# A Mamba block with a mixture of experts on one core: all eight PSUM banks in one pool, and new places for the side steps

## What is computed

```python
xz = x @ in_proj_w.T;  x_ssm, z = split(xz)
x_conv = silu(causal_conv4(x_ssm, conv_w) + conv_b)
B, C, delta = split(x_conv @ x_proj_w.T);  delta = softplus(delta)      # 16, 16, 1 columns
for t:                                                                   # per feature d, state n
    h = exp(delta * A) * h + delta * B * x_conv
    y = sum_n h * C
y = (y + D_param * x_conv) * silu(z);  return y @ out_proj_w.T

probs = softmax(tokens @ router_w.T + router_b);  two best experts of 8, weights normalised
out = sum over the two: weight * (token @ expert_weights[e])
```

## Time and profile before

| | us |
|---|---|
| median of the runs | 2801.45 (2800.16 to 2802.34, 3 runs) |
| the profiled execution | 2800.39 |
| its span, first to last instruction | 2798.2 |
| mean granted clock of PE | 0.915 of full speed |

### The profile page before, as it was taken

One profiled execution on the slowest core, in us unless ns is written; L12 is line 12 of the kernel. 1 busy time (PEld: TensorE's weight loads), 2 busy tenths in 40 slices (PEclk: granted clock), 3 DMA queues, 4 the chain that ended last, 5 costly groups with the idle time before them and its releaser, 6 DMA issues.

```text
span 2798.2 us, 34482 instructions
## 1 busy us (share of the span) xinstructions
PE 2333.2 (83%) x9510; PEld 1349.9 (48%) x9510; DVE 2258.4 (81%) x3144; ACT 1487.9 (53%) x2417; POOL 1808.3 (65%) x1418
## 2 busy tenths in 40 slices
PE   5668677698989989798988889798988989798886
PEld 2335344455545455454545455454545555454442
DVE  3789988989898989898888989888888989767300
ACT  3554555466564656466564656566474656434221
POOL 2556766657575867768676767768685767748542
PEclk8778877899999999899999999899998999899998
DMA  3772421223233443435443443435353443346866
GB/s 121 252 270 85 143 82 39 99 72 127 87 115 107 132 134 112 143 98 151 117 136 103 131 136 110 146 99 144 113 149 100 126 142 104 119 121 181 223 209 154
DMA packets 192569, 366.27 MB, mean 131 GB/s; under 512 B 22912, under 2 KB 22912, under 8 KB 192384
## 3 DMA queue, kind: packets, MB, share of 16 engines
q1 hardware_dynamic: 144272, 263.26, 28.8%
q0 software_dynamic: 28672, 67.13, 11.2%
q10 hardware_dynamic: 19440, 33.69, 3.3%
HBM read 212.73 MB, written 151.26 MB: 130 GB/s over the span
## 4 chain that ended last, share of the span: by engine, by line
PE 34%; DVE 20%; issue 18%; ACT 12%; POOL 12%; DMA 3%; SPq 0%; DVEq 0%; POOLq 0%; ACTq 0%
PE work L1191 11%; PE work L1195 10%; DVE h L1020 9%; DVE acc L1028 7%; PE hT L1206 6%; POOL u L735 5%; DVE xc L1051 3%; ACT decay L881 3%; PE work L1206 3%; PE work L1186 2%; POOL x_out L835 2%; POOL row_scratch L820 1%; POOL row_scratch L822 1%; ACT L881 1%; ACT xc L933 1%
## 5 line engine op out<-in xcount | busy, mean ns | idle before, releaser
L735 POOL TENSOR_TENSOR u<-xc,b_ring 128x1024 f32<-128x1024 f32 x512 | 1221.0, 2404 | 758.0 <-DVE h L1020 554.0
L881 ACT ACTIVATE decay<-dt,neg_a 128x512 f32<-128x512 f32 x1024 | 699.1, 689 | 603.2 <-DVE h L1020 581.3
L1206 PE MATMUL hT<-ident,h 128*128 128x128 f32 x4096 | 681.6, 298 | 349.2 <-DVE acc L1028 252.4
L1206 PEld LDWEIGHTS hT<-ident,h 128*128 128x128 f32 x4096 | 513.1, 152 | 683.2 <-DVE acc L1028 311.7
L1020 DVE TENSOR_TENSOR_SCAN h<-decay,h_last,u 128x512 f32<-128x512 f32 x512 | 651.6, 1274 | 131.8 <-ACT decay L881 85.5
L1020 DVE TENSOR_TENSOR_SCAN h<-decay,u 128x512 f32<-128x512 f32 x512 | 620.5, 1214 | 137.5 <-ACT decay L881 92.2
L1028 DVE SCALAR_TENSOR_TENSOR acc<-hT,ct,acc 128x512 f32<-128x512 f32 x960 | 697.1, 726 | 20.6 <-PE hT L1206 19.2
L1191 PE MATMUL work<-w_exp,xeT 128*128 x764 | 385.2, 628 | 34.0 <-issue 20.8
L1195 PE MATMUL work<-w_exp,xeT 128*128 x764 | 360.5, 594 | 0.0
L1191 PE MATMUL work<-xnT,w_in 128*128 128x512 f32 x512 | 261.9, 637 | 0.7 <-issue 0.7
L1195 PE MATMUL work<-xnT,w_in 128*128 128x512 f32 x512 | 241.9, 595 | 0.0
(11 more groups left out here) (149 smaller groups left out, 2193.6 us busy)
## 6 DMA issues: line engine op xcount, KB each, us to landing
b_ring<-b_scratch SPq DMA_DIRECT2D x256, 256.0 KB
xe<-row_scratch SPq DMA_DIRECT2D x165, 256.0 KB
result_scratch<-ye SPq DMA_DIRECT2D x165, 256.0 KB
row_scratch<-x_out ACTq DMA_DIRECT2D x32, 1024.0 KB, 4.7
x<-in_x SPq DMA_DIRECT2D x66, 256.0 KB, 5.1
x_scratch<-x SPq DMA_DIRECT2D x64, 256.0 KB, 2.1
xn<-in_x SPq DMA_DIRECT2D x62, 256.0 KB, 3.9
x_out<-x_scratch SPq DMA_DIRECT2D x44, 256.0 KB, 3.3
```

The lines of the kernel that those rows point to most:

```text
L735: nc.gpsimd.tensor_tensor(out=u[:, at:at + 2, :], in0=xc[:, half, 2 * k:2 * k + 2, :], in1=b_ring[:, n % ROWS:n % ROWS + 1, :].to_broadcas ...
L881: nc.scalar.activation(decay_bank[g % 2][:], dt[:, half, :], ACT.Exp, scale=neg_a[:, c, n:n + 1]).then_inc(decay_ready, 1)
L1206: last = nc.tensor.transpose(ps[:, k * P:(k + 1) * P], tile(k), ident[:])
```

## The change

One pool of eight banks takes the place of the three sets. `OWNERS` says which use a bank last had: two decay, two transposes, four products at the start. `choose` picks a bank among the idle ones. A decay or a transposed state takes one of its own, or one of the products' as long as it owns fewer than three (`RINGS` gives the least and the most). A product takes one of the products', else an idle one of a use that owns more than two, else any idle one. The first of the idle list is the one that has been free longest. What a bank's next user waits for is that bank's own last use (`wait_bank`): a scan, a sum, or a product's release. The order of `decay`, `scan`, `h_sum` and `h_T` in the list stays. The numbers of all eight tables are new; a few are shown.

```diff
@@ -52,129 +52,131 @@
     PLACES = N * C + 3
-    WORK = 4
+    BANKS = 8
+    OWNERS = ["decay"] * 2 + ["h_T"] * 2 + ["work"] * 4
+    RINGS = {"decay": (2, 3), "h_T": (2, 3)}
     HT = 2
...
-        "gather": [8.51, 14.25, 31.61, 33.76, 45.59, 48.95, 54.3, 62.45],
+        "gather": [8.8, 12.29, 29.08, 31.46, 41.89, 47.71, 54.7, 60.67],
-        "y_T": [3.7, 4.51, 4.55, 4.82],
+        "y_T": [4.43, 4.52, 4.87, 4.87],
-        "y_skip": [5.86, 5.98, 7.73, 9.62],
+        "y_skip": [5.75, 5.85, 7.57, 7.79],
-        "y_gate": [9.95, 10.13, 10.35, 10.44],
+        "y_gate": [6.67, 6.71, 10.4, 10.55],
-        "out_project": [10.17, 11.89, 14.71, 15.84],
+        "out_project": [10.75, 11.89, 14.71, 15.84],
-        "norm_stat": [4.74, 5.93, 12.25, 15.81],
+        "norm_stat": [5.92, 7.34, 15.35, 15.62],
-        "norm_rstd": [9.64, 19.17],
+        "norm_rstd": [10.21, 19.08],
-        "norm_apply": [7.43, 12.34, 18.05, 18.16],
+        "norm_apply": [10.01, 10.14, 18.01, 18.99],
-        "conv": [24.42, 25.32, 26.7, 27.51, 28.22, 29.02, 29.17, 31.14, 33.61, 34.98, 35.28, 35.75],
+        "conv": [25.96, 26.63, 26.77, 29.89, 30.06, 30.69, 33.81, 34.1, 35.13, 35.88, 36.01, 36.4],
-        "z_evict": [47.03, 49.21, 59.5, 61.93],
+        "z_evict": [48.82, 49.67, 57.75, 60.86],
-        "silu_x": [37.83],
+        "silu_x": [38.14],
-        "dt_exp": [42.94],
+        "dt_exp": [43.99],
-        "dt_plus": [42.67],
+        "dt_plus": [43.66],
-        "b_scale": [44.08],
+        "b_scale": [43.97],
-        "row_of": [40.91],
+        "row_of": [38.98],
-        "expert": [12.67, 15.33, 18.98, 27.8, 33.16, 35.02, 40.91, 47.06, 52.1, 58.89, 61.63, 65.09],
+        "expert": [13.29, 15.09, 20.77, 27.8, 32.16, 35.02, 40.91, 47.18, 52.65, 58.89, 62.04, 66.25],
-        "expert_end": [13.41, 15.35, 19, 28.22, 33.16, 35.04, 40.93, 47.08, 54.79, 58.91, 62.38, 66.67],
+        "expert_end": [14.16, 16.45, 20.89, 28.62, 33.06, 35.44, 42.33, 49.08, 56.19, 60.91, 62.38, 68.25],
-        "expert_evict": [15.73, 17.5, 23.7, 31.49, 37.48, 39, 47.74, 55.35, 58.65, 63.34, 66.63, 68.35],
+        "expert_evict": [17.5, 19.88, 25.42, 34.04, 37.55, 39.98, 51.57, 57.23, 60.02, 64.58, 67.09, 71.31],
...
@@ -294,33 +296,65 @@
 
     TAKES = {"norm_T": "norm_evict", "project": "project_out", "z_project": "z_evict", "dt_project": "dt_plus", "xp_project": "b_scale",
              "c_T": "c_evict", "y_T": "y_skip", "out_project": "residual", "norm2_T": "norm2_evict",
-             "router": "gate_logits", "rank": "row_of", "rows_T": "rows_evict", "expert": "expert_evict"}
-
-    def frees(s):
+             "router": "gate_logits", "rank": "row_of", "rows_T": "rows_evict", "expert": "expert_evict",
+             "decay": "scan", "h_T": "h_sum"}
+
+    def held(j, s):
+        if s[0] == "h_T":
+            return ("h_sum", ((j + s[3]) * N + s[1]) * Q + s[2])
+        if s[0] == "decay":
+            return ("scan",) + s[1:]
+        return TAKES[s[0]], s[1]
+
+    def frees(j, s):
+        if s[0] == "h_sum":
+            return ("h_sum", ((j + s[3]) * N + s[1]) * Q + s[2])
+        if s[0] == "scan":
+            return s
         if s[0] == "conv" and s[2] == EDGE - 1:
             return ("project_out", s[1])
         return s[:2]
 
-    def work_banks():
-        uses, idle, count, holder = {}, list(range(WORK)), [0] * WORK, {}
+    def choose(idle, owner, s):
+        of = s[0] if s[0] in RINGS else "work"
+        if of == "work":
+            long = [r for r, (least, _) in RINGS.items() if owner.count(r) > least]
+            some = [i for i in idle if owner[i] == "work"] or [i for i in idle if owner[i] in long]
+        else:
+            may_grow = owner.count(of) < RINGS[of][1]
+            some = [i for i in idle if owner[i] == of or may_grow and owner[i] == "work"]
+        i = (some or idle)[0]
+        owner[i] = of
+        return i
+
+    def bank_uses():
+        uses, idle, holder = {}, list(range(BANKS)), {}
+        count, last, owner = [0] * BANKS, [None] * BANKS, list(OWNERS)
         for j in ITERATIONS:
             for s in iteration(j):
                 if s[0] in TAKES:
                     assert idle, (j, s)
-                    bank_no = idle.pop(0)
-                    uses[j, s] = bank_no, count[bank_no]
-                    count[bank_no] += 1
-                    holder[TAKES[s[0]], s[1]] = bank_no
-                elif frees(s) in holder:
-                    idle.append(holder.pop(frees(s)))
+                    i, key = choose(idle, owner, s), held(j, s)
+                    idle.remove(i)
+                    uses[j, s] = i, count[i], last[i]
+                    if s[0] == "h_T":
+                        uses[key], last[i] = i, ("summed", key[1])
+                    elif s[0] == "decay":
+                        last[i] = "scanned", (j * N + s[1]) * C + s[2] + 1
+                    else:
+                        count[i] += 1
+                        last[i] = "free", count[i]
+                    holder[key] = i
+                elif frees(j, s) in holder:
+                    idle.append(holder.pop(frees(j, s)))
         return uses
 
-    USES = work_banks()
+    USES = bank_uses()
     STEP_IN = {(s[0], s[1]): j for j in ITERATIONS for s in iteration(j) if s[0] in EXPERTS}
 
     def use_of(j, key):
         j = STEP_IN.get(key, j)
-        return USES[j, key]
+        return USES[j, key][:2]
 
     ctx = ExitStack()
     with ctx:
@@ -429,17 +463,15 @@
         def bank(name):
             return ctx.enter_context(nc.psum_tensor(name, [P, 512], fp32))
 
-        decay_bank = [bank(f"decay{i}") for i in range(2)]
-        hT_bank = [bank(f"hT{i}") for i in range(HT)]
-        work_bank = [bank(f"work{i}") for i in range(WORK)]
+        work_bank = [bank(f"bank{i}") for i in range(BANKS)]
 
         b_dram = nc.dram_tensor("b_scratch", [2, N, T], fp32, kind="Internal").ap()
         x1_dram = nc.dram_tensor("x1_scratch", [TOKENS, D], fp32, kind="Internal").ap()
         row_dram = nc.dram_tensor("row_scratch", [2 * REGION, D], fp32, kind="Internal").ap()
         res_dram = [nc.dram_tensor(f"result_scratch{i}", [RESULTS, D], fp32, kind="Internal").ap() for i in range(3)]
 
-        work_full = [sem(f"work_full{i}") for i in range(WORK)]
-        work_free = [sem(f"work_free{i}") for i in range(WORK)]
+        work_full = [sem(f"work_full{i}") for i in range(BANKS)]
+        work_free = [sem(f"work_free{i}") for i in range(BANKS)]
         first_loaded = [sem(f"first_loaded{i}") for i in range(Q)]
         project_loaded = sem("project_loaded")
         scan_loaded = sem("scan_loaded")
@@ -561,6 +593,24 @@
             else:
                 wait(eng, summed, (block * (N - 1) + m - 1) * Q + q + 1)
 
+        def decay_bank(j, n, c):
+            return work_bank[USES[j, ("decay", n, c)][0]]
+
+        def hT_bank(k):
+            return work_bank[USES["h_sum", k]]
+
+        def wait_bank(eng, j, key):
+            i, _, last = USES[j, key]
+            if last is None:
+                return
+            kind, n = last
+            if kind == "scanned":
+                eng.wait_ge(scanned, n)
+            elif kind == "summed":
+                wait_summed(eng, n // (N * Q), n // Q % N, n % Q)
+            else:
+                eng.wait_ge(work_free[i], n)
+
         def wait_full(eng, j, key):
             bank_no, before = use_of(j, key)
             eng.wait_ge(work_full[bank_no], before + 1)
@@ -876,9 +926,8 @@
                             wait_used(act, j - 1, ("dt_project", 0))
                         if j == 0 and n == 0 and c == 0:
                             act.wait_ge(a_ready, 2)
-                        g = n * C + c
-                        wait(act, scanned, j * N * C + g - 1)
-                        nc.scalar.activation(decay_bank[g % 2][:], dt[:, half, :], ACT.Exp, scale=neg_a[:, c, n:n + 1]).then_inc(decay_ready, 1)
+                        wait_bank(act, j, s)
+                        nc.scalar.activation(decay_bank(j, n, c)[:], dt[:, half, :], ACT.Exp, scale=neg_a[:, c, n:n + 1]).then_inc(decay_ready, 1)
                     elif s[0] == "h_sum" and s[1] == 0:
                         q, i = s[2], j + s[3]
                         k = i * N * Q + q
@@ -887,7 +936,7 @@
                             wait_used(act, i - 1, ("c_T", 0))
                             if j > 0:
                                 wait_product(act, j, ("y_T", C - 1))
-                        nc.scalar.activation(acc[:, q, :], hT_bank[k % HT][:], ACT.Copy, scale=ct[:, i % 2, q, 0:1]).then_inc(first_summed, 1)
+                        nc.scalar.activation(acc[:, q, :], hT_bank(k)[:], ACT.Copy, scale=ct[:, i % 2, q, 0:1]).then_inc(first_summed, 1)
                     elif s[0] == "keep_h":
                         n = s[1]
                         act.wait_ge(scanned, (j * N + n + 1) * C)
@@ -1017,7 +1066,7 @@
                             elif half == 1:
```

(13 more changed lines are left out.)

## The result

The changed kernel takes **2771.8 us** (median; 2768.6 to 2774.1) against 2800.8 for the kernel before in the same session: ratio 0.9891, 95% interval [0.9879, 0.9904]. It is faster by 1.1%. The prediction said 2815, slower; its range of 2760 to 2845 holds the time. All medians here are over fast runs; one slow run of e5, of 7314.73 us, is left out.

The account below looks back on a forecast made before the run. PE bounds an iteration from the gates to place 28, DVE with its stalls the rest. Iterations 3 to 14 +26, 0 to 2 -5, 15 and the end -6: total +15 on 2800.4 gives 2815 us, range 2760 to 2845.

Parts of the forecast that it names:

- rival A: Places 8 to 28: late ACT evictions, not PE, set the pace, so half the stalls return; 2760 us, chance 0.25.
- Iterations 0 to 2: Early iterations: a real third decay bank returns a third of 14 us of decay stalls; -5 us, bounds -14 to 0.
- Iteration 15 and the end: Last iteration and after: a quarter of ACT's 23.9 us wait for expert products returns; -6 us, bounds -24 to +13.
- Iterations 3 to 14: Twelve steady iterations: the part-by-part terms sum to +2.2 us each, +26 us in all.
- One-bank decays: Eight bare places outside the PE stretch pay 0.25 us each; +2.0 us an iteration, bounds 0 to 6.8.
- SiLU of x: Behind decay 38 instead of before it, one more place covers ACT's block; -1.5 us an iteration, bounds -2.3 to 0.
- Softplus: After decay 43: DVE stalls 1.3 us at dt_plus and 0.7 more at decay 44; +1.5 us an iteration, bounds 0 to 3.
- PE stretch: Places 12 to 28: PE is the bound with the same matmuls and keeps what stalls give back; 0 us.
- Gates: POOL's reordered queue around place 8 ends earlier or later by at most one gate, 1.25 us; 0 us.
- Third bank for transposed states: 23 of 64 transposed states get it, against DVE's 1.2 us wait; -0.5 us an iteration, bounds -1.2 to 0.
- B: Places 8 to 12: more PE work in places 4 to 7 keeps the clock high; 32 us less, 2783, chance 0.10.
- C: One-bank decays put ACT and DVE in lockstep, every eviction wait reaching DVE; 58 us more, 2873, chance 0.12.

Follow-up runs that it names:

- e5: Changed kernel with decays held to at most two banks, transposed states still up to three; 2766.7 us, ratio 0.9867 to the kernel before.
- e14: Changed kernel's pool with all old places, decays held at two banks, transposes two to three; 2777.0 us, ratio 0.9908 to the kernel before.
- e15: Changed kernel's pool with all old places and no ring allowed to grow beyond two banks; 2801.3 us, ratio 1.0000 to the kernel before.
- e1: Changed kernel with every table of places as before, so only the pool of eight banks is new; 2773.6 us, ratio 0.9895.
- e4: Changed kernel with the four steady tables (post, prep, experts, combine) as before, new late tables kept; 2774.6 us, ratio 0.9903.
- e7: Kernel before, with eight decays in each of iterations 3 to 14 made to wait for the scan just before; 2814.8 us, ratio 1.0063.
- e12: Changed kernel with old places in iterations 3 to 13, new ones in 0 to 2, 14 and 15; 2762.3 us, ratio 0.9853 to the kernel before.
- e8: Kernel before, with 27 decays in each of iterations 3 to 14 made to wait for the scan just before; 2869.2 us, ratio 1.0244.
- e16: As e12, with y_T, y_skip and y_gate at the changed kernel's places in iterations 3 to 13 too; 2763.0 us, ratio 0.9841.
- e6: Changed kernel with transposed states held to at most two banks, decays still up to three; 2898.3 us, ratio 1.0338 to the kernel before.
- e18: As e6, with the second load of expert rows at place 8.09 instead of 7.2; 2859.3 us, ratio 1.0200 to the kernel before.
- e3: Changed kernel with new steady tables and the late tables of before; no time, since its engines wait for each other in a circle.
- e13: As e12, with decays held at two banks and transposes allowed two to four; 2779.0 us, ratio 0.9908 to the kernel before.

## Why the prediction was right and wrong

It said 2815, slower, and the kernel got faster: the profiled span fell by 31.7 us where +15 was forecast. That the time lies within its range is owed to rival A's bound, not to the forecast.

**Iterations 0 to 2: the step that failed most.** It said -5 and the trace says -23. It credited only the third bank of the decays, with a third of their stalls, and put the third bank of the transposes at nothing here. By e14 and e15 14 of the 23 us come from that bank (434.6 against 448.8), by e1, e4 and the changed kernel 4 to 7 from the new places; for the decays' bank e5 and e14 leave 2.0 and 1.3, less than equal lists differ by. The step on the transposes' bank read DVE's wait for transposed states in iteration 8, 1.2 us, counted it for iterations 3 to 14 alone, and closed with "PE gains slack that nothing waits for". But in iterations 0 to 2 of the kernel before DVE waits 11.7 us for PE's transposes (6.1 for its sums, 5.6 for its scans), and 4.9 for the out projection, which is queued among them. These are the waits that e14 takes away. The stalls for decays, on which the prediction built, stay (28.9 us in e15, 27.6 in e14).

**Iteration 15 and the end: mis-sized.** -6 forecast, -18.4 measured (-18.2 and -0.2), within the bound of -24. The term was a quarter of ACT's wait for expert products, 23.9 us; that wait fell by 15.4, to 8.5, and 17.3 of the 18.2 us came between places 12 and 28. The pool gives up to 6.4 of it (e1, though e7 shows 3.9 with nothing changed there), the rest needs the new places there; new late tables alone don't bring it (e4, 180.2), all tables of iterations 14 and 15 do (e12, 168.5). The last run of expert tiles, which PE fills, did stay as it was: the gain lies before it.

**Iterations 3 to 14: the sign right, the size under half.** +26 forecast, +10.3 measured.

- *One-bank decays.* The mechanism was right and its price at a place nearly: 2.04 us from scan to scan (1558.21 to 1560.25 to 1562.29), 0.20 more, 0.25 forecast. That PE's stretch covers them is shown by e8 (1.0 us for 12 to 28). The term, +24, was too large: eight places at 0.20 are 19, and e7 measures 14.3 in the kernel before. A decay just ahead of an absence of ACT can cost far more, 4.0 us an iteration for places 36 to 40 of e8; with the SiLU in its new place the changed kernel doesn't pay that.
- *SiLU of x.* -1.5 an iteration forecast, and right: DVE's waits for decays in places 36 to 40 fell by 20.5 us, 1.7 an iteration. These places nevertheless grew by 20.5 us in all, since two taps and `row_of` came to stand there (29.4 us more busy time of DVE) and scans 38 now wait 8.7 us for POOL's `u`, which no term had. Waits for `u` fell by 10.2 in places 50 to 64.
- *Softplus.* Right: a stall of 1.26 us before `dt_plus` (1.3 forecast; the view names no one for it, and the logarithm ends 0.10 us before the step) and 0.48 before scan 44 (0.7). Places 42 to 44 grew by 21.8 us in the twelve iterations, 4.8 of it two one-bank decays; 17.0 are left, 18 were forecast. The drain that the Trainium skill counts with a table load (ScalarE: Activation LUTs, What ACT_TABLE_LOAD costs) is not in this trace either: the load ends at 1555.53 and the logarithm begins at 1555.54. Places 40 to 50 grew by only 9.7, though this term and seven one-bank decays were to bring 39: places 40 and 49 got shorter by 6.2 and 12.3 us (place 49 from 2.63 to 1.84 us in odd iterations and from 3.04 to 1.78 in even ones), which no term had.
- *PE stretch.* PE is the bound between places 12 and 28, as said (busy 27.07 of 27.07 and 20.09 of 20.09 us). But "the same matmuls" was counted by list places, not by time: more of them now run before scan 12, and the stretch lost 25.4 us in the sum. From scan 0 to scan 28 it is 5.7, near the 0 forecast. The sign that was to prove the prediction wrong, under 45 us, came in iterations 9, 11 and 13 (43.77 in iteration 9).
- *Gates.* 0 forecast, with "earlier or later by at most one gate", 1.25 us. From scan 0, the last gate ends 0.2 us earlier in odd iterations and 2.1 us later in even ones, where the bound fails; the out projection begins 0.7 us earlier and 2.2 us later. The prediction had read iteration 8 alone. e16 shows both signs by itself, and that they cancel.
- *Third bank for transposed states.* -0.5 an iteration forecast. With the old places it is 0 (1897.7 and 1897.9 in e14 and e15); with the new ones it keeps 96 us away (e6 against the changed kernel). One term that stands by itself couldn't hold this: the new lists need the longer ring.
- *A load past another.* The prediction did not weigh `rows_load` 8.09 to 7.2. It costs 39 us if PE's queue is late (e6, e18) and is hidden here by the third bank.
- *Slips in the working.* 1.4 times the stall of 3.05 us is 4.3 and not 4.4. One of the 27 one-bank decays (place 6) lies before place 12, and five decays in each of iterations 1 and 2 have one bank too. 2406.15 is the last scan of iteration 14; iteration 15 begins at 2408.23. The stretch of the earlier trace rows reaches 4 us into places 8 to 12; ahead of scan 8 PE was busy 6.05 of 11.00 us. None of these changes a reading of the result.

**The rivals.** A (2760) and B (2783) both missed 2771.8 by 11 to 12 us. A is refuted as a reason for most of the gain, since e1 has it without the new places. Its stalls around place 18 did shrink (DVE's waits for decays in places 12 to 28 fell from 59.6 to 29.7 us), but by scan 28 only 5.7 us of it are left. B is half there: the clock at places 8 to 12 of the changed kernel is 0.90 in iteration 9, and 0.50 in iteration 8, lower than before; over the twelve iterations it rose from 0.55 to 0.65 in places 8 to 12 and fell from 0.83 to 0.79 in places 0 to 8. Its share was not isolated. C's price stands in e8, but 48.2 of its 68.5 us where ACT goes away for the SiLU, not at every eviction. No rival had a longer ring of transposes as the cause.

**What stays open.** What the clock gave; how much of iteration 15 the new steady places bring by themselves, since e3 has no time; what shortened places 40 and 49; and why a fourth bank costs time.

## What to carry to other kernels

Where one engine's queue mixes a paced job with others' work, list that engine's own waits and what waits for it, in every regime and not in one iteration only: a buffer more for the paced job brings forward all that is queued behind it, though in iteration 8 its reader hardly waited for it. Judge a borrowed buffer by when it comes free in time, not by its place in a list: a ring of one costs little at a bare place and nearly the whole absence of its writer where that goes away. Before a stretch that grew is put down to a cause, split it into busy time and waits, and count from an event that doesn't move: places 36 to 40 grew although their stall shrank, and places 8 to 28 shrank because scan 8 came later. Whenever a load is moved, look for the load that it now stands in front of.

## What the runs showed of the hardware

After idle times of 13.35 us (e5) and 13.65 us (e13) at one place of iteration 0, PE came back to the upper of its two levels (2.4 GHz, a granted clock of 1.00) at different times. Two stretches with the same eight wide matmuls, e5 and then e13 (columns as in the stretches above):

```profile
66.12:70.22 4.10, 4.10 (x9) 1.77 (x9) 1.58 (x3) 0.17 (x2) 3.05 (x2) 0.84 0.98 351
```

```profile
66.08:71.68 5.60, 5.60 (x9) 2.25 (x9) 1.58 (x3) 0.18 (x2) 3.03 (x2) 0.61 0.84 296
```

The granted clock is 0.84 in one and 0.61 in the other. It costs e13 1.5 us on PE, and DVE's next stall there is 5.40 instead of 3.90 us. This is one place in two traces, and wasn't tested by itself.
